# Moving the norms of a kernel's last stage beside its second attention

## The reference, cut to what matters

```
hn   = layernorm(x)                        # no gain, no shift
out  = attention(hn @ w_qkv) @ w_out + b_out
out  = (out - mean) / sqrt(var + 1e-6) * ln_gamma + ln_beta      # first norm
x    = x + out
xn   = (x - mean) / sqrt(var + 1e-5)                             # second norm
res  = x + (xn @ filter + bias)
```

## Time and profile before

| | |
|---|---|
| median of the runs | 2105.53 us |
| the profiled execution | 2109.18 us |
| its span, first to last instruction | 2107.5 us |
| mean granted TensorE clock | 0.914 |
| busy: PE, DVE | 1835.4 us (87%), 1692.1 us (80%) |
| busy: ACT, POOL | 1242.0 us (59%), 1132.8 us (54%) |

### The profile page before, as it was taken

How to read it: one execution, slowest core, us unless ns; L and a number is a source line. 1 busy time by engine, 2 the same in 40 slices (tenths; PEclk the granted TensorE clock), 3 DMA queues, 4 the chain that set the end, 5 groups by cost and what they waited for, 6 DMA issues and landing times. The chain is left out here.

```text
span 2107.5 us, 48492 instructions
## 1 busy us (share of the span) xinstructions
PE 1835.4 (87%) x18758; PEld 862.1 (41%) x18758; DVE 1692.1 (80%) x3207; ACT 1242.0 (59%) x2377; POOL 1132.8 (54%) x683
## 2 busy tenths in 40 slices
PE   5547756999999856969999999999999999999975
PEld 3347632233333344634442444444444444444433
DVE  7942377999999384445649999999999999999947
ACT  5412133788888601227764777777776777777655
POOL 8722552000000065320205888888888888888877
PEclk9778867899999957989997999999999999999995
DMA  1220026111111051148873223223323323322201
GB/s 47 38 44 3 0 86 232 46 47 40 45 46 47 3 171 54 52 138 316 323 297 98 67 77 82 74 70 82 79 65 82 82 65 79 82 71 73 67 11 41
DMA packets 194490, 180.18 MB, mean 85 GB/s; under 512 B 58741, under 2 KB 155125, under 8 KB 194053
## 3 DMA queue, kind: packets, MB, share of 16 engines
q1 hardware_dynamic: 185860, 170.01, 27.8%
q0 software_dynamic: 2944, 7.10, 1.0%
q10 hardware_dynamic: 5504, 0.73, 0.2%
HBM read 101.16 MB, written 75.26 MB: 84 GB/s over the span
## 5 line engine op out<-in xcount | busy, mean ns | idle before, releaser
L892 POOL TENSOR_TENSOR part_sums_l<-probs_l 128x1024 f32<-128x1024 f32 x256 | 610.3, 2384 | 206.7 <-ACT probs_l L957 196.1
L957 ACT ACTIVATE probs_l<-exp_l 128x512 f32<-128x512 f32 x1024 | 573.7, 596 | 166.6 <-PE exp_l L1005 148.8
L916 DVE TENSOR_REDUCE maxima_l<-max_l 128x1 f32<-128x512 f32 x1024 | 644.1, 679 | 4.4 <-PE max_l L994 1.6
L994 PE MATMUL max_l<-k_stack_l,q_stack_l 96*128 96x512 f16 x1024 | 399.8, 391 | 5.0 <-DVE pv_bank_l L908 2.8
L1005 PE MATMUL exp_l<-q_stack_l,k_stack_l 100*128 100x512 f16 x1024 | 390.2, 382 | 2.1 <-ACT probs_l L957 1.6
L1212 DVE TENSOR_REDUCE maxima_l<-max_l 128x1 f32<-128x512 f32 x512 | 317.1, 683 | 16.9 <-PE max_l L1298 16.7
L1249 ACT ACTIVATE probs_l<-exp_l 128x512 f32<-128x512 f32 x512 | 279.3, 599 | 59.7 <-PE exp_l L1311 55.9
L1039 PE MATMUL pv_bank_l<-probs_l,v_ring_l 128*32 128x512 f32 x2048 | 272.7, 605 | 0.3 <-issue 0.3
L994 PEld LDWEIGHTS max_l<-k_stack_l,q_stack_l 96*128 96x128 f16 x1024 | 99.7, 97 | 280.9 <-DVE maxima_l L916 216.2
L1722 POOL IOTA rows_e<- 128x32 int32 x1 | 0.2, 184 | 386.3 <-POOLq L26 386.3
L898 POOL TENSOR_TENSOR part_sums_l<-part_sums_l 128x512 f32<-128x512 f32 x128 | 184.0, 1438 | 10.0
(11 more groups left out here) (278 smaller groups left out, 2595.9 us busy)
## 6 DMA issues: line engine op xcount, KB each, us to landing
scratch_qk_l<-parts_g SPq DMA_DIRECT2D x128, 256.0 KB, 2.8
q_stack_l<-scratch_qk_l SPq DMA_DIRECT2D x192, 128.0 KB, 2.9
k_stack_l<-scratch_qk_l SPq DMA_DIRECT2D x192, 128.0 KB, 3.0
scratch_v_l<-v_g SPq DMA_DIRECT2D x16, 1024.0 KB
v_ring_l<-scratch_v_l SPq DMA_DIRECT2D x64, 256.0 KB, 3.3
scratch_stack_l<-parts_c SPq DMA_DIRECT2D x16, 384.0 KB, 3.6
q_stack_l<-scratch_stack_l SPq DMA_DIRECT2D x64, 96.0 KB, 2.2
k_stack_l<-scratch_stack_l SPq DMA_DIRECT2D x64, 96.0 KB, 2.3
```

Source lines behind the costliest of these rows:

```text
L892: pool.tensor_tensor(part_sums[:, i, h, :, :], probs[:, i, h, 0:2, :], probs[:, i, h, 2:4, :], ALU.add).then_inc(pair_sum.sem, 1)
L916: dve.reduce_max(maxima[:, s % 2, at % NT, at // NT:at // NT + 1], max_bank(n, at)[:, :], AX).then_inc(max_taken.sem, 1)
L957: act.activation(probs[:, i, at // NT, at % NT, :], exp_ps[at % 2][:, :], ACT.Exp, scale=a.scale).then_inc(prob_tile.sem, 1)
L994: pe.matmul(max_bank(n, at)[:, :], qs[0:SHIFT_ROW, s % RING, h, k * P:(k + 1) * P], ks[0:SHIFT_ROW, s % RING, h, :], start=True, stop=True ...
```

## The change

The statistics and scalings of the first norm for batches 0 to 6, the residual for them, and the statistics of the second norm for batches 0 to 5 are made in the second attention, by ACT and POOL, at places written out in two tables. A sum is made by an activation's accumulator output; so is the sum of squared deviations. The mean times -1 and the sum of squares stand for bn_stats; the square root of 128 that this leaves goes into gamma and the filter. The copy that spreads inverse sums goes from DVE (place 10) to ACT (place 11), the reciprocal from place 10 to 9, and the transposes from places 14 and 15 to 13 and 15. The filter, the loads of the rows, and the addition of beta to `g.x` go to the projections. In the last stage PE's transposes of the next batch come ahead of the products of the present one.

```diff
-SUMS_AT, SUMS_COPY_AT, SUMST_AT, INVERSE_AT, INVERSET_AT, NORMALISE_AT = 7, 7, (9, 9), 10, (14, 15), 0
+SUMS_AT, SUMS_COPY_AT, SUMST_AT = 7, 7, (9, 9)
+INVERSE_AT, INVERSE_ROWS_AT, INVERSET_AT, NORMALISE_AT = 9, 11, (13, 15), 0
+BESIDE_ACT = ({(0, at): ("sum", 0, k) for k, at in enumerate((2, 5, 9, 14))}
+              | {(1, at): ("square", 0, k) for k, at in enumerate((1, 5, 9, 13))}
+              | {(3, 5): ("shift", 0, 0), (3, 9): ("normal", 0, 0), (3, 14): ("normal", 0, 1), (4, 2): ("normal", 0, 2), (4, 5): ("normal", 0, 3)}
+              | {(6, at): ("sum", 1, k) for k, at in enumerate((2, 5, 9, 14))}
+              | {(7, at): ("square", 1, k) for k, at in enumerate((2, 5, 9, 14))}
+              | {(10, 5): ("shift", 1, 0)})
+BESIDE_POOL = {(2, 3): ("power", 0), (4, 3): ("gamma", 0), (5, 2): ("residual", 0), (8, 3): ("power", 1)}
+BESIDE_FIRST, BESIDE_SECOND = 7, 6
+def beside(table, n, at, U):
+    for (groups, place), (step, i, *tile) in table.items():
+        b, over = divmod(n - groups - OUT_LAG, U)
+        if place == at and over == 0 and 1 <= b <= (BESIDE_FIRST, BESIDE_SECOND)[i]:
+            yield (b - 1, step, i, *tile)
 # attention, POOL: called ahead of the additions of head h
+            def norms_beside(n, h):
+                for b, step, i in beside(BESIDE_POOL, n, h, U):
+                    if step == "power":
+                        pool.wait_ge(r.squared[i].sem, r.squared[i].made(b, NT - 1))
+                        pool.tensor_scalar(r.var_eps[:, i, tiles], r.squares[:, i, tiles], D * (L1_EPS, LN_EPS)[i], None, ALU.add).then_inc(r.var_ready[i].sem, 1)
+                        pool.wait_ge(r.var_ready[i].sem, r.var_ready[i].made(b, 0))
+                        pool.tensor_tensor(r.rstd[:, i, tiles], r.var_eps[:, i, tiles], g.minus_half[:, 0:NT], ALU.pow).then_inc(r.rstd_ready[i].sem, 1)
+                    if step == "gamma":      # out *= gamma, 128x512
+                    if step == "residual":   # out += g.x, 128x512
 # attention, DVE
-                        dve.wait_ge(inv_ready.sem, inv_ready.made(n - PV_LAG, 0))
-                        dve.tensor_copy(inv_rows[:, :, :, :], bc(inv_sums[:, :, :], HEAD_ROWS)).then_inc(inv_rows_ready.sem, 1)
 # attention, ACT: called last at each place, behind the exponential and the copies
+            def norms_beside(n, at):
+                for b, step, i, k in beside(BESIDE_ACT, n, at, U):
+                    if step == "sum":
+                        act.activation(r.junk[:, :], out[:, tile, :], ACT.Identity, scale=-1.0 / D,
+                                       accum_out=r.minus_mean[:, i, tile:tile + 1]).then_inc(r.summed[i].sem, 1)
+                    if step == "square":
+                        act.wait_ge(r.summed[i].sem, r.summed[i].made(b, NT - 1))
+                        act.activation(r.junk[:, :], out[:, tile, :], ACT.Square, bias=r.minus_mean[:, i, tile:tile + 1],
+                                       accum_out=r.squares[:, i, tile:tile + 1]).then_inc(r.squared[i].sem, 1)
+                    if step == "shift":      # four copies of 128x1, scale = rstd
+                    if step == "normal":     # out = out * rstd + shift, one tile
+                    if at == INVERSE_ROWS_AT and exists(turn, s, PV_LAG):
+                        act.wait_ge(inv_ready.sem, inv_ready.made(n - PV_LAG, 0))
+                        act.copy(inv_rows[:, :, :, :], bc(inv_sums[:, :, :], HEAD_ROWS)).then_inc(inv_rows_ready.sem, 1)
 # projections
+            # SP, behind w, w_out and b_out: wf (two), fourier, beta, gamma, bias
+            # POOL, for each batch behind its normalised tiles:
+                pool.tensor_tensor(x, x, beta[:, :].unsqueeze(1).broadcast_to([P, NT, D]), ALU.add).then_inc(x_beta, 1)
+            # ACT, ahead of the first copy:
+            act.wait_ge(out_loaded, 16 * 4)
+            act.mul(g.gamma[:, :], g.gamma[:, :], D ** 0.5).then_inc(gamma_scaled, 1)
+            # PE, batch 0: ahead of tile 2 filter_halves() (waits for wf), ahead of tile 6 filter_whole()
 # last stage, PE
-            for b in range(B):      # transposes of b, then products of b
+            transposes(0)
+            for b in range(B):
+                if b + 1 < B:
+                    transposes(b + 1)
+                products(b)
 # last stage, ACT
+            normal(0)
+            normal(1)
+            transposed(0)
+            first_norm()            # batch 7 alone
+            for b in range(2, B):
+                normal(b)
+                transposed(b - 1)
+            transposed(B - 1)
```

More of the change, by code:

```diff
@@ L791, with open_norms @@
 HALVES_ADD_AT = (2, 4)
-SUMS_AT, SUMS_COPY_AT, SUMST_AT, INVERSE_AT, INVERSET_AT, NORMALISE_AT = 7, 7, (9, 9), 10, (14, 15), 0
+SUMS_AT, SUMS_COPY_AT, SUMST_AT = 7, 7, (9, 9)
+INVERSE_AT, INVERSE_ROWS_AT, INVERSET_AT, NORMALISE_AT = 9, 11, (13, 15), 0
 OUT_AT = (3, 5, 13, 15)
+BESIDE_ACT = ({(0, at): ("sum", 0, k) for k, at in enumerate((2, 5, 9, 14))}
[6 more added lines that the diff above has]
+BESIDE_FIRST, BESIDE_SECOND = 7, 6
+def open_norms(nc, g, ctx):
+    sem = phase_semaphores(nc, ctx, "_norms")
+    sb = lambda name, shape: ctx.enter_context(nc.sbuf_tensor(f"{name}_norms", shape, F32))
+    made = lambda name, per=1: Product(sem(name), per)
+    r = g.norms = Shared()
+    r.minus_mean, r.squares, r.var_eps, r.rstd, r.shift = [sb(n, [P, 2, T]) for n in ("minus_mean", "squares", "var_eps", "rstd", "shift")]
+    r.junk = sb("junk", [P, D])
+    both = lambda name, per=1: [made(f"{name}{i}", per) for i in range(2)]
+    r.summed, r.squared, r.var_ready, r.rstd_ready, r.shift_ready = both("summed", NT), both("squared", NT), both("var_ready"), both("rstd_ready"), both("shift_ready")
+    r.normal, r.scaled, r.whole = made("normal", NT), made("scaled"), made("whole")
+def beside(table, n, at, U):
[3 more added lines that the diff above has]
+            yield (b - 1, step, i, *tile)
 def attention(nc, g, a, scratch, w_out, out, addend):
@@ L947, in _ @@
         def _(act):
+            r = g.norms
+            def norms_beside(n, at):
+                for b, step, i, k in beside(BESIDE_ACT, n, at, U):
+                    tile = b * NT + k
+                    if step == "sum":
+                        if k == 0 and i == 0:
+                            act.wait_ge(y_taken.sem, b + 2)
+                        if k == 0 and i == 1:
+                            act.wait_ge(r.whole.sem, r.whole.made(b, 0))
+                        act.activation(r.junk[:, :], out[:, tile, :], ACT.Identity, scale=-1.0 / D,
[5 more added lines that the diff above has]
+                    if step == "shift":
+                        act.wait_ge(r.rstd_ready[i].sem, r.rstd_ready[i].made(b, 0))
+                        for tile in range(b * NT, (b + 1) * NT):
+                            last = act.activation(r.shift[:, i, tile:tile + 1], r.minus_mean[:, i, tile:tile + 1], ACT.Copy,
+                                                  scale=r.rstd[:, i, tile:tile + 1])
+                        last.then_inc(r.shift_ready[i].sem, 1)
+                    if step == "normal":
+                        act.wait_ge(r.shift_ready[i].sem, r.shift_ready[i].made(b, 0))
+                        act.activation(out[:, tile, :], out[:, tile, :], ACT.Identity, bias=r.shift[:, i, tile:tile + 1],
+                                       scale=r.rstd[:, i, tile:tile + 1]).then_inc(r.normal.sem, 1)
             def step(turn, s):
@@ L2242, in post_l1 @@
         stored = [sem(f"stored{s}") for s in range(2)]
-        row = lambda n: rows[:, n, :].unsqueeze(1).broadcast_to([P, NT, D])
-        y = lambda b: g.y[:, b * NT:(b + 1) * NT, :]
-        x = lambda b: g.x[:, b * NT:(b + 1) * NT, :]
+        gamma, bias = (row[:, :].unsqueeze(1).broadcast_to([P, NT, D]) for row in (g.gamma, g.bias))
+        tiles_of = lambda b: slice(b * NT, (b + 1) * NT)
+        y = lambda b: g.y[:, tiles_of(b), :]
         block = ctx.enter_context(nc.Block())
@@ L2343, in _ @@
+            moments_of(1, last_b - 1)
+            centre(0, last_b)
+            centre(1, last_b - 1)
+            result(0)
+            whole()
+            moments_of(1, last_b)
+            result(1)
+            centre(1, last_b)
+            for b in range(2, B):
+                result(b)
         @block.scalar
         def _(act):
[L2345 to L2365 removed]
@@ new lines, in scaled, with normal @@
+            def scaled(i, tile):
+                return dict(bias=r.shift[:, i, tile:tile + 1], scale=r.rstd[:, i, tile:tile + 1])
+            def normal(b):
+                if (1, b) in shift_ready:
+                    act.wait_ge(shift_ready[1, b], 1)
+                if b >= 2:
+                    act.wait_ge(xnT_ps.sem, xnT_ps.made(b - 2, 0))
+                for k in range(NT):
+                    act.activation(xn[:, b % 2, k, :], g.y[:, b * NT + k, :], ACT.Identity, **scaled(1, b * NT + k)).then_inc(xn_ready.sem, 1)
@@ new lines, in transposed, with first_norm @@
+            def transposed(b):
```

(12 more changed lines are left out.)

198 lines of the change are left out of this document (99 added, 99 removed).

## The result

The changed kernel takes 2079.33 us (median of four runs, 2076.82 to 2082.65), the kernel before 2105.31 beside it. The ratio is 0.9874, 95% interval 0.986 to 0.9889: faster by 1.26%. The forecast was 2078.9. The profiled execution took 2081.31 us with a span of 2079.6, against 2109.18 and 2107.5.

What follows compares the result with a forecast made beforehand. PE, with DVE nearly full, was taken to bound the second attention, and a chain through four engines the last stage. -30.0 + 2.0 - 7.3 + 5.2 + 1.0 + 2.5 = -26.6, so 2078.9 us; range 2066 to 2095.

Steps and rivals of the forecast that it cites:

- the signs named: Last stage 26 to 31 us, head group 14.15 to 14.35, DVE about 91%, ACT near 84%, no attention table loads.
- Last stage: Final stage: PE at the low clock bounds it; 59.7 us falls to 29.7, gain 30.0, bounds 28.7 and 34.5.
- Rival A: Whole kernel: work beside the attention is free and the last stage warms up; -37.3, to 2068.2 us; chance 0.20.
- Rival D: Last stage: stays a 45 us chain, PE slow and stores holding result buffers; gain 11.3, 2094.2 us; chance 0.06.
- Projections: Projections: the filter's six products moved here show in full on busy PE; +2.0 us, bounds +1 and +5.
- The copy: Second attention: inverse-sum copy moves from DVE to ACT, PE regains 0.12 us a group over 61 groups; -7.3 us.
- The passes and GpSimd's insertions: Second attention: ACT's norm passes cost +5.2 us (0 to +15.6), POOL's insertions +1 (0 to +6).
- Its count of 26: Second attention: 26 groups with four passes, each showing 0.2 us from a pass after exponential 14; +5.2 us.
- B: Second attention: passes show and POOL holds DVE, +15.6 and +6; gain 11.2, 2094.3 us; chance 0.16.
- C: Second attention: ACT's exponentials become the bound, passes show in full, from 0.31 us each; slower, 2161.7 us; chance 0.06.
- my estimate of +15: Second attention: 12 gamma and residual operations on POOL each hold DVE 1.26 us, all passed on; 15 us instead of +1.
- Drain: After the last maxima: POOL is the bound, batch 6's gamma and residual add 2 x 1.26; +2.5 us, bounds 0 and +3.

Runs made afterwards that it cites:

- e6: Changed kernel with GpSimd's gamma and residual left out, ScalarE's work beside the attention kept: 2071.03 us, ratio 0.984 to the kernel before.

## Why the prediction was right, and where its terms were off

The whole came out as forecast because most of its terms have the right sign and cause; three of them are mis-sized by 2 us or more in this pair of profiles, and partly cancel. Of the signs named, a group takes 14.28 us, the copy on ACT 0.6, and the changed kernel loads one table. DVE's share from 1300 to 1800 us is 94.9% and not 91, ACT's 78.3 and not 84, and the last stage, 25.0, is below the 26 to 31 named.

**Last stage: right in mechanism, the wrong one of its two clocks.** The prediction gave 31.0 us for PE at the low clock and 25.2 if the clock rose some 13 us in, took 29.7, and measured is 25.0. PE in the changed kernel:

```profile
2061.84 2.07 PE L2509 MATMUL f_ps_h<-filter,xnT_h 128*128 128x128 f32 x8
...
2064.56 1.91 PE L2509 MATMUL f_ps_h<-filter,xnT_h 128*128 128x128 f32 x8
...
2066.81 1.06 PE L2509 MATMUL f_ps_h<-filter,xnT_h 128*128 128x128 f32 x8
```

The products of eight pieces take 2.07 us, and 1.06 from about 12 us in. ACT:

```profile
2061.23 0.56 ACT L2477 COPY xnT_h<-xnT_ps_h 128x512 f32<-128x512 f32 x1
2061.70 1.65 ACT L2471 ACTIVATE xn_h<-y,shift_norms,rstd_norms 128x128 f32<-128x128 f32 x4
2063.25 0.56 ACT L2477 COPY xnT_h<-xnT_ps_h 128x512 f32<-128x512 f32 x1
2063.71 1.65 ACT L2471 ACTIVATE xn_h<-y,shift_norms,rstd_norms 128x128 f32<-128x128 f32 x4
```

It goes without a gap from 2054.56 to 2072.43, at 2.01 us a batch (2.1 forecast), and PE's last products follow it, to 2073.99: ACT paces PE over nearly the whole stage. While the clock is low ACT is behind as well, by batch 7's first norm (1.64 us), so slow products cost nothing, as the run without gamma and residual bears out. The row of the kernel before that ran at the higher level at its very end pointed to this, and I gave it too little weight; the size of this term is the prediction's largest error, -4.7. Rival A's price for this stage, -34.5, was the right one.

ACT's path is not the one that ended last, by half a microsecond. That one is batch 7's own chain, which the prediction had as next in line and through 11 us in. So it was (2065.52), but the prediction did not see what stands behind it in GpSimd's stream:

```profile
2064.50 1.02 POOL rstd_norms L2392
2065.52 2.49 POOL y L2396 x2
...
2068.09 0.70 DVE res_h L2445
...
2068.80 2.38 DMA out_dram<-res_h
...
2071.31 0.70 DVE res_h L2445
2072.01 0.02 issue
2072.03 2.29 DMA out_dram<-res_h
...
2074.45 0.69 DVE res_h L2445
```

The additions of the bias for batches 2 and 3 wait for batch 7's second power, the results wait for them, and the last results follow each other so closely that a store holds their buffer. One turn of a buffer is 3.1 us (2071.31 to 2074.45), less than the 4.0 of two batches on ACT, so it is only the late start that makes the buffers tell. The length of the last such store sets the rest: 2.29 us here, and 3.16 to 4.23 in five kernels with the same last stage, which took 25.7 to 27.3. With four buffers and batch 6's two operations on DVE the chain that ended last is ACT's. Rival D is out.

**Projections: +2.0 forecast, 0.0 in this pair, and right for PE.** The filter's products cost less than said, 1.5 us instead of 2.4, since they ran at the higher clock,

```profile
937.14 0.49 PE L2298 MATMUL xnT_ps_g<-fourier_g,wf_g 128*128 128x128 f32 x2
...
937.91 0.39 PE L2301 MATMUL xnT_ps_g<-fourier_g,wf_g 128*128 128x128 f32 x2
941.75 0.49 PE L2305 MATMUL xnT_ps_g<-fourier_g,spectrum_g 128*128 128x128 f32 x2
```

0.99 us for the four halves and 0.55 for the other two. The projections' products as a whole, from the first to the last, take 1.5 longer, 166.8 instead of 165.2. But from the stage's start to the first maximum product both kernels take 183.7: `w_g` landed 1.6 us earlier, and PE began so much earlier. What let it land earlier isn't tested, and it isn't the rule. In the other eleven profiles with the same projections, `w_g`'s first product starts 7.1 to 8.8 us in (8.74 before) and the stretch takes 183.5 to 186.3. In the three of them that start as late as before, at 8.6 to 8.8, it takes 185.2, 185.9 and 186.3: 1.5 to 2.6 us more than before. ACT did wait 4.73 us for the rows' loads, and the six banks covered it.

**The copy: -7.3 forecast, -9.0 measured** by the kernel with nothing beside. The 0.12 per group were right to 0.03 in seven steps of eight (14.21 or 14.22 to 14.12). Missed was the eighth: where DVE also adds a batch's output, a step took 14.53 and now 14.12. And the 1.19 us that DVE gives up are mostly GpSimd's hold on it, as said above.

**The passes and GpSimd's insertions: +6.2 forecast, +8.0 measured.** Their error and that of the copy cancel, and the attention came out at -1.0 for -1.1. The passes are late where the prediction said, behind exponential 14, but by 0.09 to 0.19 instead of 0.2, in four places a batch, and place 13 gives back 3.3 us; in sequence they cost 0.29 and 0.38 us instead of the 0.5 taken. Its count of 26 holds by chance: the seven groups of first squares have no piece at place 14, and seven scalings have one. Gamma and residual are 2.5 us (e6), where +1 was taken for these and the powers. Some 2 us of the 8.0 are in neither. A part of them is seen on PE in the step of the second norm's power, where the sums start 1.00 us behind the product with v instead of 0.88. Of the rivals, A needs zero here and is out, B wanted +21.6 and is out, C needed 0.31 us per pass and even doubled passes show 0.14.

The Trainium skill, "ScalarE: Activation LUTs" (What ACT_TABLE_LOAD costs), leads to the 0.293 and 0.387 us estimated for the two activations alone; the trace has 0.304 and 0.401. The price of about 0.25 that I had made of it for a pass lacked the read of the accumulator, 0.2 us, of which some 0.1 shows in sequence.

DVE is held as feared. GpSimd and DVE in the group with the residual:

```profile
1465.20 1.27 POOL L936 TENSOR_TENSOR y<-y,x_res 128x512 f32<-128x512 f32 x1
1466.42 7.55 POOL L948 TENSOR_TENSOR part_sums_l<-probs_l 128x1024 f32<-128x1024 f32 x3
```

```profile
1472.88 1.65 DVE L979 TENSOR_TENSOR part_sums_l<-part_sums_l 128x512 f32<-128x512 f32 x1
```

The addition of halves takes 1.65 us instead of the 0.68 that it takes alone and ends at 1474.53; PE's sums start at 1474.63, 1.08 behind the start of its product with v, where 0.88 is usual. The insertion of 1.27 us costs the path 0.20.

The Trainium skill, "SBUF — State Buffer" (Who interferes with whom), has such two instructions exclude one another, and the held additions agree with it; my estimate of +15 from it assumed that DVE hands all of it on. Over the twelve insertions in the steps it handed on 2.5 us, a sixth.

**Drain: +2.5 forecast, +4.7 measured; its bound of +3 was wrong.** GpSimd's part was right (2.4). The second half is a consequence not thought of: behind PE's longer idle time the work on the path ran at the lower clock.

**Altogether** the terms are off by -4.7 (last stage), -2.0 (projections), -1.7 (copy), +1.8 (passes and insertions) and +2.2 (drain): the changed stretches give -31.0, the forecast said -26.6, and the medians -26.0, with -23.4 to -29.5 by the interval. That the forecast met the median within 0.5 us is therefore partly luck. No run settled the 5 us between stretches and medians. The front that both kernels share, up to DVE's first addition of the projections, ends between 917.6 and 927.0 us over the thirteen profiled executions, a spread of 9.4. This pair of profiles also has about the shortest projections and last stage that the new code shows. And the 2105.31 of the kernel before are its lowest median; elsewhere it was 2106.42 to 2109.37.

## What to carry to other kernels

Put extra work on an engine beside a full one by its places, not by its share of idle time: ACT had 29% idle, and still four pieces a batch behind the last exponential but one cost 3.3 us, which one place earlier gave back. Where a stage has two possible clocks, work out each engine's pace at both and ask which engine bounds it in each; if it is not PE, the clock doesn't matter. Follow the order of every engine's stream there: an operation that waits holds all that stand behind it. Work laid beside a loop falls into its drain too, where nothing covers it: do the last round's share elsewhere. And edits that close the same gap don't add.

## What was not expected of the hardware

- A gap of 3.50 us in PE's work, ahead of which it had been busy at the higher level, left the next three pieces at 1.93, 1.12 and 1.94 us instead of 1.06, 0.66 and 1.06. A gap of 1.08 (and 0.94 and 1.05 in two kernels above) didn't. With each pass twice the gap was 3.46, the first of the three pieces still ran in 1.07, the others took 1.12 and 1.93, and the drain was 1.0 us shorter.
- With waits of 0.68 us per batch of 3.61 PE stayed at the low level for all products of the last stage, and it rose about 12 us in where it had none.
- A DVE copy of 128x512 from one SBUF tile to another took 0.43 us with GpSimd idle and 1.19 in the full kernel; ACT takes 0.62 for it there.
- A held DVE addition (1.65 us) and a GpSimd operation in its way (1.27) cost the path 0.20 us.
